# Two attentions re-ordered by pairs of heads, with the mixture product unmasked and its bias rows on VectorE

## The chip, the cores and the metric

One core of a Trainium2 chip runs the whole kernel in one launch. The metric is the device time of that launch in microseconds, lower is better. The engines that matter are TensorE (PE; PEld is its weight load), VectorE (DVE), ScalarE (ACT), GpSimd (POOL), and SyncE's queue (SPq), which issues the loads. Each engine runs its own instruction list in order, and waits on semaphores that the others raise.

## The reference, cut to what matters

A chain of eight layers over a matrix x of 256 rows and 768 columns: four graph layers and four feed-forward layers. Two of them hold an attention of 12 heads, 64 wide. Layer L0_ffn mixes attention and a cheap path by row:

```python
normed = _ln(hidden_states, g1, b1)
scores = sigmoid(normed @ Wr + br)
_, idx = top_k(-scores, 38); attn_mask[idx] = True
q, kk, v = (normed @ W + b for each)
probs = softmax(q @ kk.T / 8); ctx = probs @ v
attn_out = ctx @ Wo + bo
pooled = (scores / sum(scores)) @ normed
mix_out = (normed + scores[..., None] * pooled) @ Wm + bm
merged = where(attn_mask, attn_out, mix_out)
h = hidden_states + merged
h = h + gelu(_ln(h, g2, b2) @ W1 + bf1) @ W2 + bf2
```

L3_ffn, the last layer, has the same attention for all rows, with low-rank additions to q, k and v, then one projection whose result is added to x.

## The kernel before, in words

The 256 rows are two halves m=0, 1 of 128 partitions. Every weight product is done in three passes on rounded parts: a weight tile (128x768) is copied by ScalarE into its upper part WH (`feed_act`, L294), VectorE subtracts to get the lower part WL (`feed_vec`, L301), and activations have upper and lower parts in XS or GS (L481 on ScalarE, L485 on VectorE). There are four places for such tiles (NPAIR = 4). `ahead(i)` feeds up to tile i+4, and a place is free when PE has used it up. Raw tiles come three at a time (a unit) from SyncE's queue in a fixed order, into six buffers. A chunk of 256 output columns takes two tiles, and for each half m it is a unit of 6 x 3 matmuls.

Stage L0_ffn runs: transposes, query and key products (`pe_gemm_T`), the scores of head pairs 0 and 1, the mask's row and columns (mrow, mT) by PE, the value product (`pe_gemm_N`, tiles fv to fv+5), the attention (`pair_pe`, `pair_act`, `pair_vec`: one instruction order for each engine), the output product "om" (tiles fom to fom+11), layer norm, and the two feed-forward products. Of the eight PSUM banks, scores have 0 to 3, the turned exponentials 4 and 5, the context 6, and the spread of the reciprocals 7. `bank_at` makes PE wait until a bank's last content has been read.

For pair i of heads: `pair_scores` (PE, 8 instructions); minima of the scores (they are computed negated) by VectorE, `pair_least` (L1368); `pair_exp` (ScalarE, L1337) with the row sums in `rs`; `turn_p` (PE transposes, L363), copies of the turned halves by ScalarE (L474) and VectorE (L477); reciprocals of the sums (L1387), times the mask in L0 (L1390); `spread` (PE, L1304), which lays them along the rows; `mix` (PE, L1316), the product with the values; `ctx` (L1379), their product; then its upper (L481) and lower part (L485). The order on PE for step i is

```python
turn_p(i); spread(i)
if i + 2 < 6: pair_scores(a, i + 2, ...)
if i: mix(i - 1)
```

On VectorE it is reciprocal i, lower i-2, copy i, minima i+2, ctx i-1; on ScalarE copy i, rows i, exponentials i+2, upper i-1.

The masks: the reciprocals are multiplied by the mask column, so that the attention half is zero in rows that don't want it. The mixture mixT is multiplied by the inverse mask's row mrow on GpSimd (L1694), which also makes its lower part (L1696). "om" is one sum in PSUM for each chunk: mixture half (GS), a product of the two mask columns mT (2 partitions) with the two bias rows, and attention half (XS). VectorE adds it to xn3 (L1669).

Of the kernel before, what the change touches and what calls it, by code (L numbers as in the profile page):

```python
# [5 lines left out]
P = 128  # L6
# [148 lines left out]
def build(nc, dr, out, qgr):  # L155
    ctx = ExitStack()
    with ctx:
# [1109 lines left out]
        class Pairs:  # L1267


            def __init__(self, name, E, PT, RB, CT):  # L1270
                self.name, self.RB, self.CT = name, RB, CT
                self.E = [t.rearrange("p (h m n) -> p h m n", h=2, m=2) for t in E]
                self.PT = [t.rearrange("p (h k n) -> p h k n", h=2, k=2) for t in PT]
                self.least = [sm((name, "least", i), 4) for i in range(2)]
                self.rs = [sm2((name, "rs", i), 2) for i in range(2)]
# [11 lines left out]
        def pair_pe(a, qTv, kTv, vv, free):  # L1287
# [11 lines left out]
            def spread(i):  # L1299
                b = bank_at(7, (n + "rb", i), (act, n + "rb", i))  # L1300
                T.wait_ge(vec, n + "rs", i)
                for m in range(2):
                    for h in range(2):
                        ins = T.e.matmul(b[64 * h:64 * h + 64, m * P:(m + 1) * P],  # L1304
                                         a.rs[i % 2][:, m, h:h + 1].broadcast_to((P, 64)), ident,
                                         start=True, stop=True, skip_group_check=True)
                ins.then_inc(*pe(n + "rb", i))
# [12 lines left out]
            for i in range(6):  # L1320
                turn_p(i)
                spread(i)
                if i + 2 < 6:
                    pair_scores(a, i + 2, qTv, kTv, free)
                if i:
                    mix(i - 1)
            mix(5)

        def pair_exp(a, i):
            n = a.name  # L1330
            A.wait_ge(vec, n + "least", i)
            if i >= 2:
                A.wait_ge(pe, n + "tp", i - 2, 1)
            for h in range(2):
                bv = ps(n + "sc", i, h).rearrange("p (m n) -> p m n", m=2)
                for m in range(2):
                    A.e.activation(a.E[i % 2][:, h, m, :], bv[:, m, :], ACT.Exp, bias=a.least[i % 2][:, 2 * h + m:2 * h + m + 1],  # L1337
                                   scale=-1.0, accum_out=a.rs[i % 2][:, m, h:h + 1]).then_inc(*act(n + "E", i, h, m))

        def pair_act(a, beside):  # L1340
            n = a.name

# [4 lines left out]
            for i in range(6):  # L1347
                A.wait_ge(pe, n + "tp", i, 0)
                if i >= 2:
                    A.wait_ge(pe, n + "mix", i - 2)  # L1350
                act_copy(a.PT[i % 2][:, 0, :, :], two(ps(n + "tp", i, 0)), n + "pt", i)
# [3 lines left out]
                act_copy(a.RB[i % 2], ps(n + "rb", i)[:, 0:256], n + "rb", i)  # L1355
                if i + 2 < 6:
                    pair_exp(a, i + 2)
                if i:
                    upper(i - 1)
# [11 lines left out]
        def pair_vec(a, keep=None):  # L1371
# [12 lines left out]
            for i in range(6):  # L1384
                r = a.rs[i % 2]
                V.wait_ge(act, n + "E", i, 1, 1)
                V.e.reciprocal(r, r).then_inc(*vec())  # L1387
                if keep is not None:
                    V.wait_ge(vec)
                    V.e.tensor_tensor(r, r, keep.broadcast_to((P, 2, 2)), ALU.mult).then_inc(*vec())  # L1390
                vec.also(n + "rs", i)
                if i >= 2:
                    lower(i - 2)
                V.wait_ge(pe, n + "tp", i, 1)
                if i >= 2:
                    V.wait_ge(pe, n + "mix", i - 2)
                vec_copy(a.PT[i % 2][:, 1, :, :], two(ps(n + "tp", i, 1)), n + "pt", i)
                if i + 2 < 6:
                    pair_least(a, i + 2)
                if i:  # L1400
                    ctx(i - 1)
# [12 lines left out]
        mrow = wk(2304, n=256)  # L1414
        mT = wk(2816, n=256)
# [7 lines left out]
        def l0ffn_sync():  # L1423
# [3 lines left out]
            load_row("f0bom", 768, (pe, "sel2", 31, 2), parts=2)  # L1427
# [3 lines left out]
        def l0ffn_pe():  # L1431
# [22 lines left out]
            mk2 = sm("mk2", 4)  # L1454
            T.wait_ge(vec, "mk2")
            b = bank_at(4, ("mrow",), (vec, "mrow"))
            for m in range(2):
                ins = tr(b[:, m * P:(m + 1) * P], mk2[:, 2 * m + 1:2 * m + 2].broadcast_to((P, P)))
            ins.then_inc(*pe("mrow"))
            b = bank_at(5, ("mT",), (vec, "mT"))  # L1460
            for m in range(2):
                ins = mm(b[0:2, m * P:(m + 1) * P], [(mk2[:, 2 * m:2 * m + 2], ident)])
            ins.then_inc(*pe("mT"))
            turn[0] = 6
            pe_gemm_N("f0v", fv, 6, 512, xs_at, lambda c, m: (vec, "f0v", c, m))
            turn[0] = 4
            pe_gemm_N("f0v", fv + 4, 6, 256, xs_at, lambda c, m: (vec, "f0v", c, m), c0=512)
            T.wait_ge(vec, "f0v", 512, 1)
            pair_pe(att0, f0qA, f0kA, f0vA, there)
            turn[0] = 0  # L1470
            i = fom
            for c in range(0, 768, 256):
                h = c % 512
                if h == 0:
                    ob = [bank(("om", c, m), (vec, "hx", c, m)) for m in range(2)]
                for part_ in range(2):
                    T.wait_ge(lo, "w", i + 1)
                    if part_ == 0:
                        T.wait_ge(pool, "lower", "mix")
                    wh, wl = (v.rearrange("p (t k c) -> p t k c", t=2, k=6) for v in (w_hi(i, 2), w_lo(i, 2)))  # L1480
                    for m in range(2):
                        o = ob[m][:, h:h + 256]
                        ms = slice(m * P, (m + 1) * P)
                        for k in range(6):
                            if part_:
                                T.wait_ge(vec, "lower", "f0ctx", k)
                            x = (xs_at if part_ else gs_at)(k)
                            ins = mm(o, three_N(wh[:, :, k, :], wl[:, :, k, :], (x[0][:, ms], x[1][:, ms])),
                                     part_ == 0 and k == 0, part_ == 1 and k == 5, True)
                        if part_ == 0:  # L1490
                            T.wait_ge(*row_sem("f0bom"))
                            T.wait_ge(vec, "mT")
                            ins = mm(o, [(mT[0:2, ms], row("f0bom")[0:2, c:c + 256])], False, False, True)
                        ins.then_inc(*pe("om", c, part_, m))
                    for j in (i, i + 1):
                        pe.also("w", j)
                    i += 2
# [35 lines left out]
        def l0ffn_act():  # L1533
# [22 lines left out]
            feed_act(ahead(fv + 4))  # L1556

            def beside(i):
                if i == 2:
                    A.wait_ge(pool, "mix")  # L1560
                    act_upper(GSv[:, 0, :, :], mixT, "mix")
# [5 lines left out]
            affine_act("nT1", "f0g2", "f0b2", (pe, "om", 512, 1, 1))  # L1567
# [9 lines left out]
        def l0ffn_vec():  # L1577
# [41 lines left out]
            for m in range(2):  # L1619
                vec_gemm(fk, 2 * m + 2, None, 2 * m)  # L1620
# [10 lines left out]
                V.e.tensor_reduce(rk[:, m:m + 1], Gt, AX.X, ALU.add).then_inc(*vec())  # L1631
            mkv = mk2.rearrange("p (m a) -> p m a", m=2)
# [3 lines left out]
            vec_gemm(fk, 6, None, 4)  # L1636
            for k in range(6):
                V.wait_ge(vec, "pooled")
                V.e.scalar_tensor_tensor(out=mixT[:, k, :], in0=srow, scalar=pooled[:, k:k + 1], in1=nT[:, k, :],
                                         op0=ALU.mult, op1=ALU.add).then_inc(*vec("mixT", k))  # L1640
# [7 lines left out]

            feed_vec(ahead(fv))
            pair_least(att0, 0)  # L1650
            pair_least(att0, 1)
            V.wait_ge(pe, "mrow")
            V.e.tensor_copy(mrow, ps("mrow")[:, 0:256]).then_inc(*vec("mrow"))
            V.wait_ge(pe, "mT")
            V.e.tensor_copy(mT[0:2, :], ps("mT")[0:2, 0:256]).then_inc(*vec("mT"))
# [4 lines left out]
            pair_vec(att0, mkv[:, :, 0:1])  # L1660
            for c in range(0, 768, 256):
                feed_vec(ahead(fom + c // 256 * 4))
                feed_vec(ahead(fom + c // 256 * 4 + 2))
                if c:
                    c0 = c - c % 512
                    for m in range(2):
                        V.wait_ge(pe, "om", c, 1, m)
                        V.wait_ge(pool, "lower", "mix")
                        V.e.tensor_tensor(hx[:, m, c0:c + 256], ps("om", c0, m)[:, 0:c + 256 - c0], xn3[:, m, c0:c + 256],  # L1669
                                          ALU.add).then_inc(*vec("hx", c0, m))  # L1670
            vec_ln("f0c", hx, xn3, D, lambda m: V.wait_ge(vec, "hx", 512, m))
            affine_vec("nT1", "f0g2", "f0b2", (pe, "om", 512, 1, 1))
# [16 lines left out]

        def l0ffn_pool():  # L1690
            G.wait_ge(vec, "f0v", 512, 1)
            G.wait_ge(vec, "mixT", 5)
            G.wait_ge(vec, "mrow")
# [1488 lines left out]
```

## Time and profile before

| what | us |
|---|---|
| median of 3 runs | 1433.06 (1428.75 to 1434.76) |
| profiled execution, its own time | 1437.31 |
| its span in the trace | 1435.4 |
| PE busy | 1342.3 |
| DVE busy | 970.9 |
| ACT busy | 775.6 |
| POOL busy | 207.1 |

The span is what the trace covers; the execution's own time has a little around it. Busy time of one engine says how much of the span it works, not whether it sets the end. The first attention lies at about 545 to 590 us of the span, its output product at 590 to 621, and the last attention at 1379 to 1418.

### The profile page before, as it was taken

To read this page: it belongs to the slowest core of one execution; us is meant where nothing else is said; L and a number is where in the kernel's file an instruction comes from. 1 tells how busy PE (TensorE), PEld (TensorE's weight loads), DVE (VectorE), ACT (ScalarE), POOL (GpSimd) and SP (SyncE) were. 2 spreads that over 40 slices of the span, in tenths; PEclk is the share of its full clock that TensorE was granted. 3 is DMA by queue.
4 is the path that set the end of the run, shared out by engine and by line. 5 is a ranking of instruction groups with operands and counts; after the bars stand their busy time and mean duration, and the time that the engine had idled before them with its cause. 6 is when DMAs were issued, how large, how long until landed. Compare 5 with 4: busy or idle time off the path is not lost.

```text
span 1435.4 us, 24144 instructions
## 1 busy us (share of the span) xinstructions
PE 1342.3 (94%) x10078; PEld 1152.6 (80%) x10078; DVE 970.9 (68%) x1703; ACT 775.6 (54%) x1259; POOL 207.1 (14%) x103
## 2 busy tenths in 40 slices
PE   9999999999999889888799999789999999998798
PEld 8999543799633587787698999769899999987786
DVE  8745777745777767566667767776677767767454
ACT  3445888535888555454545554634445554436344
POOL 0110776100586200002001000001000000000100
PEclk9999999999999999999899999899999999998899
DMA  9456364135464123045233453063454555132200
GB/s 355 108 199 189 99 188 122 67 132 166 132 188 131 61 84 121 1 152 199 90 153 135 159 184 133 23 242 129 139 196 167 178 191 194 67 158 96 78 1 23
DMA packets 30835, 194.82 MB, mean 136 GB/s; under 512 B 4211, under 2 KB 4339, under 8 KB 14726
## 3 DMA queue, kind: packets, MB, share of 16 engines
q1 hardware_dynamic: 30726, 193.27, 39.6%
q8 instruction: 80, 1.31, 0.4%
q14 instruction: 29, 0.24, 0.1%
HBM read 183.03 MB, written 3.93 MB: 130 GB/s over the span
## 4 chain that ended last, share of the span: by engine, by line
PE 73%; DVE 15%; ACT 6%; POOL 3%; issue 2%; DMA 0%; DVEq 0%; SPq 0%; ACTq 0%
PE PS L358 56%; PE PS L979 6%; PE PS L988 5%; PE PS L363 3%; DVE WL L301 3%; POOL WK L1174 2%; PE PS L619 1%; POOL WL L308 1%; DVE SM L535 1%; ACT WH L294 1%; ACT WK L1337 1%; DVE GS L485 1%; ACT GS L481 1%; DVE WK L1810 1%; DVE WK L2683 1%
## 5 line engine op out<-in xcount | busy, mean ns | idle before, releaser
L301 DVE TENSOR_TENSOR WL<-w,WH 128x768 fp32r<-128x768 f32 x373 | 356.6, 967 | 204.2 <-ACT WH L294 201.3
L294 ACT ACTIVATE WH<-w 128x768 fp32r<-128x768 f32 x381 | 315.6, 840 | 256.4 <-PE PS L358 242.4
L358 PE MATMUL PS<-XS,WH 128*128 128x256 f32 x2292 | 420.8, 286 | 14.5 <-DVE XS L485 7.4
L358 PEld LDWEIGHTS PS<-XS,WH 128*128 128x128 f32 x2292 | 358.4, 191 | 18.8 <-issue 11.4
L358 PE MATMUL PS<-XS,WL 128*128 128x256 f32 x1146 | 325.6, 284 | 0.0
L358 PEld LDWEIGHTS PS<-XS,WL 128*128 128x128 f32 x1146 | 219.3, 191 | 0.0
L1112 DVE TENSOR_TENSOR WK<-PS,WK 128x1024 f32<-128x1024 f32 x128 | 156.6, 1223 | 55.5 <-ACT PS L1056 54.5
L1174 POOL TENSOR_TENSOR WK<-WK 128x1024 f32<-128x1024 f32 x64 | 152.6, 2388 | 207.9 <-ACT WK L1053 207.9
L358 PE MATMUL PS<-WH,GS 128*128 128x256 f32 x864 | 161.1, 284 | 4.6 <-issue 1.4
L1056 ACT ACTIVATE PS<-PS 128x1024 f32<-128x1024 f32 x128 | 129.5, 1011 | 34.3 <-PE PS L979 34.3
L358 PEld LDWEIGHTS PS<-WH,GS 128*128 128x128 f32 x864 | 135.9, 190 | 7.7 <-issue 4.5
L979 PE MATMUL PS<-RT,PK 128*128 128x512 f32 x384 | 122.6, 427 | 0.2
L358 PE MATMUL PS<-WL,GS 128*128 128x256 f32 x432 | 122.3, 283 | 0.0
L979 PEld LDWEIGHTS PS<-RT,PK 128*128 128x128 f32 x384 | 62.3, 188 | 71.4 <-DVE WK L1112 54.0
L358 PE MATMUL PS<-WH,XS 128*128 128x256 f32 x552 | 109.7, 285 | 1.8 <-DVE XS L485 1.8
L1982 POOL TENSOR_TENSOR XT<-XS 128x512 f32<-128x512 f32 x9 | 13.4, 1522 | 667.0 <-DVE XS L485 667.0
L988 PE MATMUL PS<-WK,cp 128*32 128x384 f32 x1024 | 107.9, 497 | 1.5 <-POOL WK L1174 1.4
L358 PEld LDWEIGHTS PS<-WH,XS 128*128 128x128 f32 x552 | 88.2, 188 | 4.4 <-issue 3.3
L358 PEld LDWEIGHTS PS<-WL,GS 128*128 128x128 f32 x432 | 82.0, 190 | 0.0
L363 PE MATMUL PS<-cp,WK 128*128 128x128 f32 x332 | 56.9, 306 | 24.7 <-ACT WK L1785 9.4
L363 PEld LDWEIGHTS PS<-cp,WK 128*128 128x128 f32 x332 | 41.7, 156 | 44.3 <-ACT WK L1785 10.9
L358 PE MATMUL PS<-WK 64*128 64x256 f32 (+4 forms) x356 | 68.9, 374 | 3.0 <-ACT WK L474 2.2
(271 smaller groups left out, 2000.3 us busy)
## 6 DMA issues: line engine op xcount, KB each, us to landing
w<-f2W_in SPq DMA_DIRECT2D x40, 1152.0 KB, 5.5
w<-Wrel_in SPq DMA_DIRECT2D x12, 1152.0 KB, 7.3
WK<-qrep_in SPq DMA_DIRECT2D x16, 768.0 KB, 5.6
w<-f1Wi_in SPq DMA_DIRECT2D x8, 1152.0 KB, 5.1
w<-f1Wo_in SPq DMA_DIRECT2D x8, 1152.0 KB, 5.1
w<-f3Wqkv_in SPq DMA_DIRECT2D x6, 1152.0 KB, 14.1
RT<-qg_rows SPq DMA_DIRECT2D x16, 384.0 KB, 6.4
RT<-AS SPq DMA_DIRECT2D x32, 192.0 KB, 6.6
```

Of the source, the lines that this page charges most:

```text
L294: A.e.activation(w_hi(i), w_raw(i), ACT.Copy).then_inc(*hi("w", i))
L301: V.e.tensor_tensor(w_lo(i), w_raw(i), w_hi(i), ALU.subtract).then_inc(*lo("w", i))
L308: G.e.tensor_tensor(w_lo(i), w_raw(i), w_hi(i), ALU.subtract).then_inc(*log("w", i))
L358: ins = T.e.matmul(o, l, r, start=i == 0 and first, stop=i == n - 1 and last, skip_group_check=lint)
L363: return T.e.transpose(o, i, ident[0:n, 0:n])
L481: A.e.activation(h, src, ACT.Copy).then_inc(*act("upper", *name))
L485: V.e.tensor_tensor(l, src, h, ALU.subtract).then_inc(*vec("lower", *name))
L979: ins = T.e.matmul(o, PK[:, j * P:(j + 1) * P], GR[b % 2][:, c:c + 512], start=True, stop=True)
L988: ins = T.e.matmul(o[32 * g:32 * (g + 1), 0:384], zsum[:, 28 - 4 * j:60 - 4 * j], SG[p % NSG][:, u, 384 * g:384 * (g + 1)], start=j == 0, ...
L1056: A.e.activation(SP[q], SP[q], ACT.Sigmoid).then_inc(*act("sig" + n, p, q))
L1112: V.e.tensor_tensor(SG[p % NSG][:, q // 2, 0:1024], SP[q], GQ[p // 4 % 2][:, 0:1024], ALU.mult).then_inc(*vec("prod" + n, p, q))
L1174: G.e.tensor_tensor(s, s, GQ[p // 4 % 2][:, 1024:1536].unsqueeze(1).broadcast_to((P, 2, 512)), ALU.mult).then_inc(*pool("prod" + n, p, 1))
```

## The change

In both attentions: PE does the scores of pair i+2 ahead of the turn of pair i; the third chunk of the value product lies between turn 0 and spread 0, with scores 2 ahead of turn 0; VectorE has the reciprocals and the minima at the head of a step; ScalarE has exponentials i+2 ahead of the rows' copy; the sums have three buffers instead of two. In L0 besides: mrow and mT are gone, and the mixture is not masked, but its product (omB, with one part ahead of the last `mix` and the rest behind it) is multiplied by the mask column when VectorE reads it from PSUM. Its upper and lower parts are made by ScalarE and VectorE before the attention, and GpSimd has no work there. The attention half (omA) has PSUM banks of its own. The bias rows are two rows broadcast to all partitions, which VectorE multiplies by the mask columns and adds. The host packs the mixture's weights ahead of the attention's.

```diff
@@ pair_pe
-            for i in range(6):
+            pair_scores(a, 2, qTv, kTv, free)
+            turn_p(0)
+            rest_v()
+            spread(0)
+            for i in range(1, 6):
+                if i + 2 < 6:
+                    pair_scores(a, i + 2, qTv, kTv, free)
                 turn_p(i)
                 spread(i)
-                if i + 2 < 6:
-                    pair_scores(a, i + 2, qTv, kTv, free)
-                if i:
-                    mix(i - 1)
+                if i == 1:
+                    T.wait_ge(vec, n + "v", 512, 1)
+                mix(i - 1)
+                beside(i)
             mix(5)
@@ pair_act
+            rows(0)
+            for i in range(1, 6):
+                pair_copy(a, i)
                 if i + 2 < 6:
                     pair_exp(a, i + 2)
-                if i:
-                    upper(i - 1)
+                rows(i)
+                upper(i - 1)
                 beside(i)
@@ pair_vec
+            for i in range(1, 6):
+                pair_shares(a, i, keep)
+                if i + 2 < 6:
+                    pair_least(a, i + 2)
+                pair_out(a, i)
                 if i >= 2:
                     lower(i - 2)
-                ...
+                ctx(i - 1)
+                beside(i)
@@ l0ffn_sync
-            load_row("f0bom", 768, (pe, "sel2", 31, 2), parts=2)
+            L.wait_ge(pe, "sum2", 31, 1)
+            L.e.dma_start(bo, dr["f0bo"].partition_broadcast(P)).then_inc(*row_sem("f0bom")[0]())
+            load_row("f0bom", 768)
@@ l0ffn_pe (beside(5) is mixed(0, 0))
-            mk2 = sm("mk2", 4)
-            ... (mrow and mT by PE)
+            pair_pe(att0, f0qA, f0kA, f0vA, there, rest_v, beside)
+            mixed(256, 0)
+            mixed(512, 2)
+            for c in range(0, 768, 256):
+                om("omA", fom + 6, c, 4 if c < 512 else 6, xs_at, lambda c, m: (vec, "hx", c, m),
+                   lambda k: T.wait_ge(vec, "lower", "f0ctx", k))
@@ l0ffn_act (beside(5) is feed_act(ahead(fom)))
+            for k in range(0, 6, 2):
+                A.wait_ge(vec, "mixT", k + 1)
+                act_upper(pair_of(GSv, 0, k), mixT[:, k:k + 2, :], "mix", k)
@@ l0ffn_vec
+            rank(0)
+            for f in range(6):
+                vec_gemm(fk, f + 1, None, f)
+                V.wait_ge(vec, "pooled")
+                V.e.scalar_tensor_tensor(out=mixT[:, f, :], in0=srow, scalar=pooled[:, f:f + 1], in1=nT[:, f, :],
+                                         op0=ALU.mult, op1=ALU.add).then_inc(*vec("mixT", f))
+            rank(1)
+            ...
+            pair_least(att0, 0)
             feed_vec(ahead(fv))
-            pair_least(att0, 0)
             pair_least(att0, 1)
+            for k in range(0, 6, 2):
+                vec_lower(pair_of(GSv, 1, k), mixT[:, k:k + 2, :], pair_of(GSv, 0, k), "mix", k)
             feed_vec(ahead(fv + 2))
             v_out(0, 512)
+            pair_least(att0, 2)
+            pair_shares(att0, 0, mkv[:, :, 0:1])
             feed_vec(ahead(fv + 4))
+            pair_out(att0, 0)
             v_out(512, 768)
+            pair_vec(att0, beside, mkv[:, :, 0:1])
+            feed_vec(ahead(fom + 2))
+            biases(0)
+            biases(1)
+            feed_vec(ahead(fom + 4))
+            V.wait_ge(vec)
+            mixed_out(0, 512)
+            feed_vec(ahead(fom + 6))
+            mixed_out(512, 768)
+            feed_vec(ahead(fom + 8))
+            om_out(0, 512)
+            feed_vec(ahead(fom + 10))
+            om_out(512, 768)
@@ biases
+            def biases(m):
+                V.wait_ge(*row_sem("f0bom"))
+                for a, b, x in ((0, bo, xn3), (1, row("f0bom")[:, 0:768], hx)):
+                    V.wait_ge(vec)
+                    V.e.scalar_tensor_tensor(out=hx[:, m, :], in0=b, scalar=mkv[:, m, a:a + 1],
+                                             in1=x[:, m, :], op0=ALU.mult, op1=ALU.add).then_inc(*vec())
@@ l0ffn_pool (whole function removed)
@@ l1gnn_sync
             load_row("g1br2", 768, (vec, "f0v", 512, 1))
-            load_row("g1be2", 768, (pe, "om", 512, 0, 1))
+            load_row("g1be2", 768, (pe, "omA", 512, 1))
             load_units(w1 + 10)
```

## Rows read from the trace of the kernel before

**Rows 1.** The page: busy time of each engine, and the last chain by engine.
```profile
PE 1342.3 (94%) x10078; PEld 1152.6 (80%) x10078; DVE 970.9 (68%) x1703; ACT 775.6 (54%) x1259; POOL 207.1 (14%) x103
PE 73%; DVE 15%; ACT 6%; POOL 3%; issue 2%; DMA 0%; DVEq 0%; SPq 0%; ACTq 0%
```
**Rows 2.** Busy time by stretches: stretch, length, engines, PE's granted clock, DMA.
```profile
554.10:589.70 35.60, 28.70 (x215) 20.37 (x213) 22.38 (x37) 17.45 (x52) 6.86 (x2) 0.86 0.15 53
589.70:620.50 30.80, 30.80 (x231) 27.96 (x230) 13.44 (x17) 11.28 (x15) 0.00 (x0) 1.00 0.10 32
1394.40:1418.00 23.60, 20.20 (x177) 13.47 (x177) 13.10 (x27) 14.38 (x49) 0.00 (x0) 1.00 0.01 2
```
**Rows 3.** PE's timeline, first attention: start, length, [idle before, releaser].
```profile
544.68 0.43 PE L363 MATMUL PS<-cp,SM 128*128 128x128 f32 x2
...
545.57 0.39 PE L358 MATMUL PS<-WH,XS 128*128 128x256 f32 x1
...
559.16 1.09 PE L363 MATMUL PS<-cp,WK 128*128 128x128 f32 x8 [0.52 <-DVE WK L1646]
562.68 1.12 PE L1304 MATMUL PS<-cp,SM 128*64 128x128 f32 x8 [2.43 <-DVE SM L1390]
563.73 2.08 PE L358 MATMUL PS<-WK 64*128 64x256 f32 x8
...
582.88 1.12 PE L1304 MATMUL PS<-cp,SM 128*64 128x128 f32 x8 [2.04 <-ACT WK L474]
```
**Rows 4.** Busy time by short stretches, first attention; PE's granted clock is third last.
```profile
558.00:560.00 2.00, 1.48 (x14) 1.28 (x12) 1.28 (x3) 0.15 (x1) 0.82 (x1) 1.00 0.32 126
...
562.60:564.00 1.40, 1.32 (x10) 0.99 (x12) 0.62 (x2) 0.15 (x1) 0.01 (x1) 0.50 0.00 0
```
**Rows 5.** Timelines of VectorE and of GpSimd, first attention.
```profile
559.22 3.40 DVE L1390 TENSOR_TENSOR SM<-SM 128x4 f32<-128x4 f32 x1
...
580.47 2.26 DVE L1390 TENSOR_TENSOR SM<-SM 128x4 f32<-128x4 f32 x1
...
559.18 3.42 POOL L1694 TENSOR_TENSOR WK<-WK 128x1536 f32<-128x1536 f32 x1 [80.12 <-DVE SM L1387]
```
**Rows 6.** The chain that ended last, at both attentions: start, length, what.
```profile
589.81 30.74 PE PS L358 x228
...
1402.06 1.93 ACT WK L1337 x8
...
1405.36 1.14 DVE SM L1368
...
1406.52 1.93 ACT WK L1337 x8
...
1418.05 13.03 PE PS L358 x108
```
**Rows 7.** PE's timeline, last attention: scores, mix, and the next scores.
```profile
1399.62 1.13 PE L358 MATMUL PS<-WK 64*128 64x256 f32 x8
1400.69 1.08 PE L1316 MATMUL PS<-WK 128*64 128x256 f32 x8
...
1403.31 1.13 PE L358 MATMUL PS<-WK 64*128 64x256 f32 x8
```
**Rows 8.** Groups by line and shape, whole span: busy us, mean ns.
```profile
L301 DVE TENSOR_TENSOR WL<-w,WH 128x768 fp32r<-128x768 f32 x373 | 356.6, 967 | 204.2 <-ACT WH L294 201.3
L294 ACT ACTIVATE WH<-w 128x768 fp32r<-128x768 f32 x381 | 315.6, 840 | 256.4 <-PE PS L358 242.4
...
L2188 DVE SCALAR_TENSOR_TENSOR WK<-WK,SM,r 128x768 f32<-128x768 f32 x2 | 1.9, 1014 | 0.0
```
**Rows 9.** Timelines of SyncE's queue and of ScalarE, around the output product.
```profile
523.50 14.19 SPq L320 DMA_DIRECT2D w<-f0Wom_in  x3
...
616.10 0.33 SPq L339 DMA_DIRECT2D r<-g1be_in  x1
...
638.00 0.83 ACT L294 ACTIVATE WH<-w 128x768 fp32r<-128x768 f32 x1
```

More of the change, by code:

```diff
@@ L1337, in pair_exp, with pair_copy, rows @@
                     A.e.activation(a.E[i % 2][:, h, m, :], bv[:, m, :], ACT.Exp, bias=a.least[i % 2][:, 2 * h + m:2 * h + m + 1],
-                                   scale=-1.0, accum_out=a.rs[i % 2][:, m, h:h + 1]).then_inc(*act(n + "E", i, h, m))
+                                   scale=-1.0, accum_out=a.rs[i % 3][:, m, h:h + 1]).then_inc(*act(n + "E", i, h, m))
+        def pair_copy(a, i):
+            n = a.name
+            A.wait_ge(pe, n + "tp", i, 0)
+            if i >= 2:
+                A.wait_ge(pe, n + "mix", i - 2)
+            act_copy(a.PT[i % 2][:, 0, :, :], two(ps(n + "tp", i, 0)), n + "pt", i)
         def pair_act(a, beside):
             n = a.name
-            def upper(i):
-                A.wait_ge(vec, n + "ctx", i)
-                act_upper(XSv[:, 0, i, :], a.CT[i % 2], n + "ctx", i)
[L1347 to L1351, printed above, removed]
+            def rows(i):
                 A.wait_ge(pe, n + "rb", i)
@@ L1463, in l0ffn_pe @@
-            ins.then_inc(*pe("mT"))
             turn[0] = 6
             pe_gemm_N("f0v", fv, 6, 512, xs_at, lambda c, m: (vec, "f0v", c, m))
[L1466 to L1469, printed above, removed]
-            turn[0] = 0
[L1471 to L1497, printed above, removed]
@@ L1556, in l0ffn_act @@
             feed_act(ahead(fv + 4))
+            pair_copy(att0, 0)
+            pair_exp(att0, 2)
             def beside(i):
-                if i == 2:
-                    A.wait_ge(pool, "mix")
-                    act_upper(GSv[:, 0, :, :], mixT, "mix")
+                if i == 5:
+                    feed_act(ahead(fom))
             pair_act(att0, beside)
@@ L1618, in l0ffn_vec, with rank @@
             V.e.tensor_copy(scol, ps("scol")[:, 0:256:128]).then_inc(*vec("scol"))
-            for m in range(2):
-                vec_gemm(fk, 2 * m + 2, None, 2 * m)
+            def rank(m):
                 sc = scol[:, m:m + 1]
@@ L1656, in l0ffn_vec, with beside @@
             feed_vec(ahead(fv + 2))
             v_out(0, 512)
+            pair_least(att0, 2)
+            pair_shares(att0, 0, mkv[:, :, 0:1])
             feed_vec(ahead(fv + 4))
+            pair_out(att0, 0)
             v_out(512, 768)
[L1660 to L1670, printed above, removed]
+            def beside(i):
+                if i == 5:
+                    feed_vec(ahead(fom))
@@ L1688, in l0ffn_vec @@
             vec_gemm_N("f0d", fw1 + 3, 3, 768, down)
[L1690 to L1693, printed above, removed]
-            G.e.tensor_tensor(mixT, mixT, mrow.unsqueeze(1).broadcast_to((P, 6, 256)), ALU.mult).then_inc(*pool("mix"))
-            G.wait_ge(act, "upper", "mix")
-            G.e.tensor_tensor(GSv[:, 1, :, :], mixT, GSv[:, 0, :, :], ALU.subtract).then_inc(*pool("lower", "mix"))
         class Gat:
@@ L3015, in pool_program @@
             l0gnn_pool()
-            l0ffn_pool()
             l1gnn_pool()
```

129 lines of the change are left out of this document (76 added, 53 removed).

## The prediction

> **What bounds the kernel now.** I read the page first: TensorE (PE) is busy 94% of the span and carries 73% of the chain that ended last [rows 1]. So a microsecond counts only where PE waits, where it runs slowly, or where it has instructions that the change takes away. Next the busy time by stretches [rows 2]. The first attention takes 35.6 us from the end of value columns 0 to 511 to the start of its output product. PE is busy for 28.7 of them at a mean granted clock of 0.86. The output product behind it is PE alone for 30.8 us, at clock 1.00. The last attention takes 23.6 us, 20.2 busy, at 1.00. The two attentions run the same code, so the last one shows what the first would cost without its extra trouble.
>
> PE's timeline of the first attention shows that trouble [rows 3]: 0.52 us for the last value evacuation, 2.43 us for the tiny masked multiply of L1390, then eight score matmuls in 2.08 us where the last attention needs 1.07 (start to start, [rows 7]), and later 2.04 us for an exponential and its copies. The granted clock behind the first idle stretch is 0.50, the 1.2 GHz level; it is 1.00 before the stretch [rows 4]. The multiply of 128x4 elements took 3.40 us, while GpSimd ran its 3.42 us product of the mixture; another took 2.26 us under GpSimd's second pass [rows 5].
>
> The chain shows the steady loop of the last attention [rows 6]: exponentials at 1402.06, minima at 1405.36, exponentials again at 1406.52. One pair costs 4.46 us and the chain goes around through ScalarE and VectorE: exponentials, upper part, lower part, copy of the turned half, minima, exponentials. PE's own instructions for a pair (scores, mix, turn, spread) take 1403.31 - 1399.62 = 3.69 us, of which the scores are 1.07 [rows 7].
>
> **Part 1, mask row and mask columns off PE.** The transposes and small products for mrow and mT begin at 544.68 and the value product at 545.57 [rows 3]. They go: 0.9 us. The value product then needs tile fv+3 two units of 2.17 us later (part 2), at 549.0. ScalarE makes that tile's upper part behind the mixture's three upper copies of 128x512, each about two thirds of the 0.84 of a 128x768 copy [rows 8], 1.7 us together; I get 547.4 for it, and 548.3 for VectorE's lower part, with the second rank (2.4 us) and the first minima ahead of it. This is hidden with 0.7 us to spare, and costs up to 0.7 if the order slips by twice that. The mixture's three lower parts on VectorE, two thirds of 0.967 each, come behind that tile, under the value product, where both engines have gaps. The row of bo and that of bm are loaded around 505, and the queue's next weight loads were at 523.5 anyway [rows 9], so the new wait ahead of them has nothing urgent behind it.
>
> **Part 2, the first attention.** PE's work: six pairs of 3.69 less the two scores done before, 6 x 3.69 - 2 x 1.07 = 20.0 us. One 128x256 unit of a weight product is 13.03 / 6 = 2.17 us at full clock [rows 6], so value columns 512 to 767, now between turn 0 and spread 0, are 4.3. Spread 0 takes bank 7, which the value product of m=1 has just left: its evacuation costs the same 0.5 us as before. No other wait remains if the loop is PE's. I followed one step of the new order with the rows' times, from the start of scores i+2 at 0. PE ends scores at 1.07, turn at 2.1, spread at 2.7, mix i-1 at 3.7. VectorE has the minima at 2.3, its copy at 2.9, ctx at 4.15. ScalarE has the exponentials from 2.35 to 4.3, rows at 4.6, upper at 4.95, and its next copy can't start before 5.3, when turn i+1 has a half. ScalarE is busy about 3.1 and VectorE about 2.7 us per step, PE 3.7. The circle of before is cut since minima stand ahead of the copy and of the lower part, and scores a turn earlier. The last mix hides its bank wait behind 4.3 us of mixture product. So the stretch from 554.2 (545.57 and four units of 2.17) to 589.7, 35.5 us, becomes 4.3 + 20.0 + 0.5 = 24.8: a gain of 10.7. Included are the clock loss (eight matmuls at 2.08 instead of 1.07, and their like) and GpSimd's hold on VectorE, since GpSimd has nothing here any more. What remains idle is as short as in the last attention, where the clock stayed 1.00.
>
> **Part 3, the output product.** It took 30.74 us [rows 6] for twelve units and six bias rows. Twelve units are 2 x 13.03 = 26.1, so the bias rows were 4.7 us and go. In their place VectorE gets four 128x768 operations with a scalar, 1.01 us each by the nearest row [rows 8]; the nearest below is the plain subtraction of 0.967. They depend on each other, so 4.2 us together. Where they lie: from the end of the last mix, ctx and upper take 0.9, ScalarE's two tiles 1.6, VectorE has its two tiles at 3.5, the biases until 7.7, and tiles fom+6, fom+7 until 9.6. PE needs them after two chunks, 8.6. It waits 1.0 us ahead of the attention half. Bounds: 0 if ScalarE and VectorE are a little quicker, 1.5 if each bias costs 1.15. After it VectorE's queue (two evacuations, each under the 1.01 us of 768 columns, and two tiles of 0.967 per chunk of 4.3) keeps ahead. The tail after the last matmul is as before: one 128x256 addition, then the statistics. Gain 3.7.
>
> The row load of g1be2 now waits for the very last unit. It went at 616.10, some 4.3 us ahead of the product's end; the weights of the next layer are queued behind it. Their first tile is used at 638.00 [rows 9], 17.4 us after that end, and such a load lands in 6 to 8 us. It is hidden; without that cover it could cost up to 4.3.
>
> **Part 4, the last attention.** Before: 23.6 us. After: 20.0 for the pairs, 0.5 for bank 7 at spread 0, 0.5 ahead of the last mix, whose bank waits for ctx 4 with nothing to put between: 21.0. Its value columns move but cost the same. Gain 2.6.
>
> **Sum.** 0.9 + 10.7 + 3.7 + 2.6 = 17.9 us. The profiled execution took 1437.3 us (span 1435.4), so 1419.4. The median of the runs shown is 1433.06, 0.3% below the profiled one; scaled by that, 1415.2.
>
> **Rule against it.** The loop still changes banks between short groups of matmuls with waits of about 0.5 us. In the last attention 3.4 us of idle time in such waits left the clock at 1.00 [rows 2]. The Trainium skill (TensorE: Matmul & The Clock Gate, section "A second HAM failure mode: psum-queue depth-cycling") says that short idle times between groups, bank after bank, can make the clock swing between its levels. This is rival B; by the rule the sum would be about 12, by the rows 17.9.
>
> **Rivals.** A: the loop stays a circle of 4.46 us (a dependence that I misjudge, say upper i-1 ahead of the next copy). Then steps 1 to 3 lose 0.77 each in both attentions, 4.6 us: gain 13, about 1420. For it: before, no middle step ran at PE's pace for long; against it: the step at 1399.62 did, as soon as minima were early. B: the clock falls once behind each of the two longer waits of the first attention (spread 0, and the 1.0 us ahead of the attention half). Rows 3 and 4 price a fall: six microseconds at half speed lose 3. Two cost 6: gain 12, about 1421. Against it: these waits are 0.5 and 1.0 us, those that were followed by a fall 2.43 and 2.04. C, slower: the clock stays at 0.50 through the first attention and its output product. This is 20 + 4.3 + 26 us of PE work, each costing as much again, 50 us at worst. It decides from 18 us of such work on, and from 25 on the kernel is slower by over 0.5%: about 1440 for 25. For it speaks only that the fall at 562.6 lasted six microseconds with PE at work; against it, the output product ran at 1.00 throughout. D: the gain is not on the end's path, so that the next stage waits for its weights: then parts 1 to 3 are cut by what the loads lag. Next-layer loads would have to be 11 us late to start to cost, and 22 to leave only 0.5%. About 1428 then.
>
> **Chances.** Forecast 0.72, A 0.12, B 0.09, C 0.02, D 0.05. A run of the kernel before varied by 0.4%, and about 0.5% is what a measurement can tell from no change. Faster by over 0.5% (below 1425.9) is the forecast, A, B: 0.93. D mostly falls within 0.5%: 0.05. Slower 0.02. The range: the low end has no wait ahead of the attention half (1.0), another microsecond of the bank waits and a median 0.3% lower (4), 1409; the high end takes in A and B, 1422.
>
> **What would show it.** No GpSimd work and no multiply over 0.2 us in 540 to 600; scores to scores 3.7 us in steps 1 to 3 of both attentions; granted clock 1.00 from the value product to the layer norm; twelve units in about 26 us with one gap of about 1 us, its releaser the lower part of a weight tile. The prediction is wrong if a step takes over 4 us, if that gap passes 2 us, or if ScalarE waits for landed weights after the stage.

## The result, and the profile after

| what | before | after |
|---|---|---|
| median, us | 1433.12 (4 runs) | 1410.34 (4 runs) |
| profiled execution | 1437.31 | 1411.12 |
| its span | 1435.4 | 1409.3 |
| mean granted clock of PE | 0.967 | 0.976 |
| PE busy | 1342.3 | 1324.7 |

The ratio is 0.9831 (95% interval 0.9809 to 0.9854): 1.7% faster, where 1.2% was forecast. 0.9831 of 1433.1 is 1408.9, just under the range's low end of 1409; the median itself, 1410.34, lies above it. A second set of six runs gave 1411.74 and 0.9866 (0.9836 to 0.9896). With all runs of this study, 80 of before (mean 1432.7, from 1424.6 to 1439.3) and 10 of the changed kernel (mean 1410.6), the gain is 22 us, give or take 2.5 (95%, from the spread of the runs). The sum said 17.9. So the direction is right and the size is some 4 us short.

Busy time by stretches of the changed kernel (stretch, length, PE, PEld, DVE, ACT, POOL, granted clock, DMA), which answers to [rows 2, 4]:

```profile
558.50:575.00 16.50, 15.95 (x152) 11.38 (x152) 11.54 (x27) 11.83 (x39) 0.00 (x0) 1.00 0.08 25
575.00:581.00 6.00, 6.00 (x50) 5.07 (x47) 2.71 (x5) 1.89 (x3) 0.00 (x0) 1.00 0.01 3
...
588.00:592.00 4.00, 3.34 (x28) 3.13 (x27) 4.00 (x6) 1.58 (x2) 0.00 (x0) 1.00 0.00 0
592.00:603.00 11.00, 11.00 (x94) 11.00 (x93) 7.29 (x11) 4.65 (x6) 0.00 (x0) 1.00 0.01 1
```

PE is busy all but half a microsecond of the loop, the clock stays at 1.00, and GpSimd has nothing. The one visible gap lies in 588 to 592. PE's timeline of the first attention, which answers to [rows 3, 7]:

```profile
558.98 0.66 PE L1304 MATMUL PS<-cp,SM 128*64 128x128 f32 x8 [0.52 <-DVE WK L1668]
559.57 1.13 PE L358 MATMUL PS<-WK 64*128 64x256 f32 x8
...
563.11 1.13 PE L358 MATMUL PS<-WK 64*128 64x256 f32 x8
...
565.68 1.03 PE L1316 MATMUL PS<-PK_,WK 128*64 128x256 f32 x8
566.65 1.14 PE L358 MATMUL PS<-WK 64*128 64x256 f32 x8
...
590.23 0.39 PE L358 MATMUL PS<-WH,XS 128*128 128x256 f32 x1 [0.66 <-DVE WL L301]
```

Spread 0 waits 0.52 us for the value evacuation, as forecast. From scores to scores is 3.54 us, less than the 3.69 counted: with the mix directly ahead of the next scores it takes 0.97 us from start to start instead of the 1.01 it took ahead of a turn, and the spread ahead of the mix takes 0.48 instead of 0.59. The wait ahead of the attention half is there, with the releaser that was named: by the spacing of its matmuls PE could have gone on at 589.4, and it did at 590.23 (the profile counts 0.66 us, from the last one's modelled end). VectorE's timeline shows why, and answers to [rows 5, 8]:

```profile
559.05 0.16 DVE L1399 TENSOR_TENSOR SM<-SM 128x4 f32<-128x4 f32 x1
...
584.26 1.01 DVE L1707 SCALAR_TENSOR_TENSOR WK<-WK,SM,XN 128x768 f32<-128x768 f32 x1
585.31 1.02 DVE L1707 SCALAR_TENSOR_TENSOR WK<-r,SM,WK 128x768 f32<-128x768 f32 x1
586.36 1.02 DVE L1707 SCALAR_TENSOR_TENSOR WK<-WK,SM,XN 128x768 f32<-128x768 f32 x1
587.42 1.02 DVE L1707 SCALAR_TENSOR_TENSOR WK<-r,SM,WK 128x768 f32<-128x768 f32 x1
588.35 1.82 DVE L301 TENSOR_TENSOR WL<-w,WH 128x768 fp32r<-128x768 f32 x2
```

The masked multiply takes 0.16 us. The four bias operations take 4.2 us, and behind them come the two tiles, ready at 590.2, that PE waits for. The chain of the changed kernel, at both attentions (start, length, what), answers to [rows 6]:

```profile
575.34 4.47 PE PS L358 x36
579.81 1.04 PE PS L1316 x8
...
590.23 13.24 PE PS L358 x108
...
1374.64 1.06 PE PS L358 x8
...
1378.17 1.06 PE PS L358 x8
...
1390.38 0.44 DVE WK L1410
1390.81 0.04 issue
1390.86 1.08 PE PS L1316 x8
```

The mixture's first part (575.34) covers what the last mix waits for in the first attention; in the last attention that wait is bare at 1390.38. The bias rows are gone from PE. In the kernel before, its timeline shows one of the six like this:

```profile
591.86 0.28 PE L358 MATMUL PS<-WH,GS 128*128 128x256 f32 x1
592.07 0.69 PE L358 MATMUL PS<-r,WK 2*128 2x256 f32 x2
592.70 0.39 PE L358 MATMUL PS<-WH,GS 128*128 128x256 f32 x1
```

The matmul ahead of it hands over 0.12 us after its start, as its neighbours do, so a bias row took 0.72 us, and six took 4.3, not the 4.7 of the forecast.

To set traces side by side I use four marks on ScalarE, its loads of function tables: ahead of the first attention (543.35 in before), behind its output product (617.76), behind the layer norm's statistics (623.50) and in the feed-forward part (643.34); and the last such load (1341.33), in the last layer, up to the span's end. Between these, in us:

| trace | 543 to 618 | 623 to 643 | 1341 to end | all the rest |
|---|---|---|---|---|
| before | 74.4 | 19.8 | 94.1 | 1247.1 |
| after | 58.9 | 18.3 | 90.8 | 1241.3 |

The first stretch gained 15.5 us and the last 3.3. The forecast had 15.3 (0.9 + 10.7 + 3.7) and 2.6. What is left, 7.3 us of 26.1, lies in places that the change doesn't touch, but for 0.1 to 0.2 us between the output product and the statistics' next mark (5.73 and 5.74 us in the traces of before, 5.60 and 5.55 in those of the changed kernel). In the feed-forward part the instructions are the same and the granted clock isn't. Here is PE alone (stretch, length, busy, granted clock, DMA), first before, then after:

```profile
628.90:632.90 4.00, 3.93 (x23) 0.65 0.24 99
```
```profile
611.80:615.80 4.00, 3.91 (x33) 1.00 1.01 414
```

23 matmuls in these 4 us at 0.65, 33 at 1.00. The question for the experiments was whether the change brings this or chance.

### The profile page after: what moved, and what is told of

Its sections match the earlier page's. It is cut to its first block, busy times and chain, and to the rows that moved or that the text cites. A ratio compares the mean times of both kernels' runs of the same rounds, so it can differ in the third digit from the quotient of the medians.

```text
span 1409.3 us, 24136 instructions
## 1 busy us (share of the span) xinstructions
PE 1324.7 (94%) x10060; PEld 1141.2 (81%) x10060; DVE 970.9 (69%) x1712; ACT 775.6 (55%) x1261; POOL 200.3 (14%) x101
## 4 chain that ended last, share of the span: by engine, by line
PE 73%; DVE 16%; ACT 6%; POOL 3%; issue 2%; DMA 0%; DVEq 0%; SPq 0%; ACTq 0%
PE PS L358 56%; PE PS L979 6%; PE PS L988 5%; DVE WL L301 3%; PE PS L363 3%; POOL WK L1174 2%; PE PS L619 2%; POOL WL L308 1%; ACT WH L294 1%; DVE SM L535 1%; DVE WK L1849 1%; ACT WK L1824 1%; DVE WK L1854 1%; DVE GS L485 1%; ACT GS L481 1%
## 5 line engine op out<-in xcount | busy, mean ns | idle before, releaser
L358 PEld LDWEIGHTS PS<-XS,WH 128*128 128x128 f32 x2292 | 355.8, 190 | 18.5 <-issue 11.1
L979 PEld LDWEIGHTS PS<-RT,PK 128*128 128x128 f32 x384 | 62.3, 188 | 71.2 <-DVE WK L1112 53.9
L358 PE MATMUL PS<-WK 128*128 128x64 f32 (+4 forms) x356 | 67.3, 366 | 3.0 <-ACT WK L474 2.2
```

What stands on the lines that cost most here:

```text
L358: ins = T.e.matmul(o, l, r, start=i == 0 and first, stop=i == n - 1 and last, skip_group_check=lint)
L979: ins = T.e.matmul(o, PK[:, j * P:(j + 1) * P], GR[b % 2][:, c:c + 512], start=True, stop=True)
```

## The experiments

Theory P: the change's own stretches give 18 to 19 us. The rest is taken to be PE's granted clock behind idle stretches elsewhere; where it is back up depends on when PE's work arrives there, not on what the change altered. Rivals: the clock is chance alone (then it averages out); or something that the change altered (loads, bank order) keeps the clock up.

**E1, E2. Both kernels again, unchanged.** No edit.

> The kernel before, unchanged, as a control. The change's own stretches explain 19 us of the 26 between the two traces; 7 us lie in stretches that it doesn't touch, where PE's granted clock rises sooner. Theory P (chance): where the clock rises differs from execution to execution. Then this trace differs from the first one of before by 1 us or more in at least one untouched stretch (the first feed-forward product behind the layer norm took 8.18 us at clock 0.79, full clock would be 6.7; the last layer's start at 1325 to 1340 ran at 0.50), and the spans of its runs spread by 4 us or more with the clock. Theory S (the change brings it): those stretches show the same clocks as in the first trace within 0.3 us, and the median stays at 1433 with the mean clock at 0.967 within 0.002.

> The changed kernel again. Theory P: mean clock of the runs 0.976 to 0.982 as before, the untouched stretches differ from the first trace of the changed kernel by 1 us or more somewhere, while value product to end of the output product stays at its 61 us within 0.3. Median 1409 to 1414. Theory S: feed-forward product at 6.67 us and the last layer's start as in the first trace, within 0.3 us.

E1: 1432.33 us (12 runs, 1425.5 to 1438.3), ratio 1.000 (0.998 to 1.002). E2: 1411.74 us (6 runs, 1405.8 to 1416.5). Stretches of E1: 73.3, 19.8, 96.5; of E2: 58.8, 18.3, 90.9. So one kernel's executions differ by over 1 us at several places, and spread by 13 us; in 35 runs of before the time is shorter where the mean clock is higher (correlation -0.91). So the clock does differ from execution to execution, as P needs, and four runs against four can't size a gain of 18 us to 2 us.

Part of the first attention's gain is such a difference. E1's first stretch is 1.1 us shorter than the first trace's. PE waits the same 2.43 us ahead of spread 0, but the spread behind the wait still runs at full speed (0.66 us, where it took 1.12), so less work falls into the slow time.

In the feed-forward stretch, 19.8 in both traces of before and 18.3 in both of the changed kernel seem to speak against chance alone. Two pairs are few, though, and elsewhere the two traces of the changed kernel don't agree. Here is PE between the same two table loads, in the first trace and in E2 (stretch, length, busy, granted clock, DMA):

```profile
746.04:768.00 21.96, 19.78 (x154) 0.92 0.24 95
```
```profile
744.25:764.65 20.40, 18.22 (x154) 1.00 0.27 103
```

The same kernel, the same 154 matmuls, 1.56 us apart.

**E3. The new order alone**, in both attentions; masks, GpSimd and output product as before.

```diff
# the changed pair_pe, pair_act, pair_vec in the kernel before; the rest of its first layer kept:
             pair_pe(att0, f0qA, f0kA, f0vA, there, rest_v, none)
             A.wait_ge(pool, "mix")        # as before, at step 2
             act_upper(GSv[:, 0, :, :], mixT, "mix")
```

> Only the new order by pairs, in both attentions; mask row, GpSimd's masking, bias rows and output product as before. My theory: steps of the pair loop at 3.5 us instead of 4.46, last attention 3.3 us shorter. In the first attention GpSimd's two passes are still there, 3.4 us each, and hold VectorE's little multiply: one wait of 1 to 3 us on PE. 1433 less 10 to 13: 1420 to 1423. Rival (the order was not what counted, only GpSimd and the bias rows did): last attention within 0.5 us of before, time 1430 or more.

1424.46 us (10 runs), ratio 0.9942 (0.9922 to 0.9962). The stretches: 69.1 in the first layer, 5 us less than in before, and 90.9 at the end, 3.2 less. GpSimd still holds VectorE up, first in the little multiply and then in the lower part of a context. PE's timeline, GpSimd's and VectorE's:

```profile
563.65 0.66 PE L1304 MATMUL PS<-cp,SM 128*64 128x128 f32 x8 [0.88 <-DVE SM L1399]
...
576.01 1.10 PE L1304 MATMUL PS<-cp,SM 128*64 128x128 f32 x8 [2.74 <-DVE SM L1399]
576.83 1.98 PE L1316 MATMUL PS<-PK_,WK 128*64 128x256 f32 x8
```
```profile
560.05 3.43 POOL L1723 TENSOR_TENSOR WK<-WK 128x1536 f32<-128x1536 f32 x1 [80.69 <-DVE SM L1396]
571.53 3.44 POOL L1725 TENSOR_TENSOR GS<-WK,GS 128x1536 fp32r<-128x1536 f32 x1 [8.05 <-ACT GS L481]
```
```profile
560.09 3.41 DVE L1399 TENSOR_TENSOR SM<-SM 128x4 f32<-128x4 f32 x1
...
571.56 3.69 DVE L485 TENSOR_TENSOR XS<-AhT,XS 128x256 fp32r<-128x256 f32 x1
...
575.70 0.16 DVE L1399 TENSOR_TENSOR SM<-SM 128x4 f32<-128x4 f32 x1
```

Two waits of 0.88 and 2.74 us, the second followed by matmuls at half speed (a mix in 1.98 us). The multiply that releases spread 4 takes 0.16 us itself. It stands behind the lower part, which took 3.69 us beside GpSimd's second pass and takes 0.41 otherwise. The order alone pays less than expected (8 to 9 us, not 10 to 13), since that pass falls where the loop has no slack.

**E4. The mixture part alone**: unmasked product, bias rows on VectorE, split output product, no GpSimd; pairs in the old order.

```diff
# the old pair_pe, pair_act, pair_vec in the changed kernel, with beside(i) at each step's end:
                 if i:
                     mix(i - 1)
+                beside(i)
             mix(5)
```

> Only the unmasked mixture, the bias rows on VectorE, the split output product, no GpSimd work; the pairs in the old order in both attentions. My theory: first attention as long as the last one of before (23.3 us of pairs), output product 26 us plus a wait of 0.8: gain 0.9 + 7.6 + 3.9 = 12.4, about 1421. No masked multiply over 0.2 us. Rival (the order is what gives the gain, GpSimd's hold would move on to another wait): under 7 us of gain, 1426 or more.

1416.52 us (6 runs), ratio 0.9900 (0.9873 to 0.9926). The first stretch is 62.3, 11 to 12 us less than before; the last is 94.1, as in before. The feed-forward stretch came out at 19.6.

**E5. Before, without GpSimd.** VectorE masks the mixture and makes its lower part. ScalarE's upper copy of the mixture moves too, from step 2 of the loop to ahead of it.

```diff
-            G.e.tensor_tensor(mixT, mixT, mrow.unsqueeze(1).broadcast_to((P, 6, 256)), ALU.mult).then_inc(*pool("mix"))
+            V.e.tensor_tensor(mixT, mixT, mrow.unsqueeze(1).broadcast_to((P, 6, 256)), ALU.mult).then_inc(*vec("mix"))
...
-            G.e.tensor_tensor(GSv[:, 1, :, :], mixT, GSv[:, 0, :, :], ALU.subtract).then_inc(*pool("lower", "mix"))
+            # at steps 2, 3, 4 of pair_vec, k = 0, 2, 4
+            V.e.tensor_tensor(GSv[:, 1, k:k + 2, :], mixT[:, k:k + 2, :], GSv[:, 0, k:k + 2, :],
+                              ALU.subtract).then_inc(*vec("lower", "mix", k))
...
-                if i == 2:
-                    A.wait_ge(pool, "mix")
-                    act_upper(GSv[:, 0, :, :], mixT, "mix")
-            pair_act(att0, beside)
+            A.wait_ge(vec, "mix")
+            act_upper(GSv[:, 0, :, :], mixT, "mix")
+            pair_act(att0, none)
```

> The kernel before with one thing changed: the mixture is masked and its lower part made by VectorE instead of GpSimd (one 128x1536 product ahead of the attention, three 128x512 subtractions in VectorE's idle time of the pair loop); the upper copy by ScalarE moves ahead of the loop. Order of the pairs, bias rows and output product as before. My theory: GpSimd's two passes cost more than half of what the mixture part gives: the 2.4 and 2.0 us waits of PE and the low clock behind them (2 to 4.5 us). From value product to the end of the output product 73.9 us becomes 66 to 68, gain 6 to 8, about 1425 to 1427; no little multiply over 0.2 us. Rival (the masked multiply was only slow because something else held VectorE, or the clock falls anyway): gain under 3, about 1431.

1425.08 us (9 runs), ratio 0.9943 (0.9924 to 0.9962): 8 us, as much as the whole new order gave, though VectorE does more. The group of the little multiplies on VectorE (count, busy, mean ns) and PE's longest wait in the loop:

```profile
L1390 DVE TENSOR_TENSOR SM<-SM 128x4 f32<-128x4 f32 x6 | 1.0, 163 | 0.2
```
```profile
568.13 0.66 PE L1304 MATMUL PS<-cp,SM 128*64 128x128 f32 x8 [0.70 <-DVE SM L1390]
```

163 ns each, where the mean of before was 1052. The first stretch is 67.3. So from 73.9 (mean of two traces of before) three steps lead down: without GpSimd 67.3, with the mixture part 62.3, with the new order 58.8: 6.5, 5.1 and 3.4 us. Each is the difference of one or two traces, and traces of one kernel differed by 1.1 us here. The 6.5 isn't GpSimd's alone: in the kernel before, ScalarE's copy of the mixture (1.49 us at 577.71) stood ahead of a copy for which PE waited 0.69 us. Up to that much, and what it cost in clock, comes from moving that copy; the two weren't tried apart.

**E6. Two of the four bias operations earlier**, at step 5 of the changed kernel.

```diff
                 if i == 5:
                     feed_vec(ahead(fom))
+                    biases(0)
...
             feed_vec(ahead(fom + 2))
-            biases(0)
             biases(1)
```

> The changed kernel with the two bias operations of m=0 moved ahead, between tiles fom+2, fom+3 and the last ctx, where VectorE was idle for 1.7 us. My theory (VectorE's four bias operations hold the tiles fom+6 and fom+7 up): the 0.66 to 0.9 us wait of PE ahead of the attention half goes, ctx 5 comes up to 0.5 us later behind cover, value product to end of output product 58.8 becomes 58.0. Rival (the wait is ScalarE's two tiles): it stays. Neither can be told by the median, 1410 to 1411; the trace decides.

1411.20 us (6 runs), ratio 0.9858 (0.9829 to 0.9887). In its chain one run of PE from 581.14 to the end of the output product has no gap:

```profile
580.13 1.01 PE PS L1316 x8
581.14 21.57 PE PS L358 x180
```

The first stretch is 57.9, 0.9 less: the four bias operations were what PE waited for. The median doesn't show it. And the feed-forward stretch came out at 19.7 instead of 18.3, with PE's clock at 0.60 at its start:

```profile
611.10:615.10 4.00, 3.96 (x21) 0.60 1.01 408
```

These are the same instructions with the same loads in the background, and more was lost there than was won.

**E7, E8. Idle matmuls behind the transposes** of six layer norms, in the changed kernel and in that of E6.

```diff
             pe_to_T("nT1", ...)
+            warm_again("f0c", 6)        # six idle matmuls in the warm-up's bank; two at five other layer norms
```

> The changed kernel with idle matmuls added behind the transposes of six layer norms, while PE waits for the parts of its input: six of about 0.44 us in the first feed-forward layer, two at five other places. Theory P: what lies outside the change's own stretches is how soon PE's clock is back up behind such idle stretches, so with the idle stretches filled it stays up more often: mean clock of the runs 0.982 or more, median 1405 to 1409. Rival (the added matmuls delay the products, or the clock falls for another reason): mean clock as before, 0.972 to 0.981, median 1411 or more.

> Both of the last two together, as a candidate that beats the changed kernel. If both theories hold: 1404 to 1408. If only the bias one: 1410.

1410.61 us (6 runs) and 1413.19 us (6 runs); mean clocks 0.975 and 0.973, no higher than the 0.977 of E2. The feed-forward stretch was 18.3 in both; in E8 that is 1.4 less than in E6, which lacks the idle matmuls. But other stretches were slow instead: the one that lies at 744 to 765 in E2, 20.40 there and in E6, took 21.93 and 21.94. Filling these small gaps isn't worth anything measurable, and this prediction of P failed. E8 doesn't beat the changed kernel.

**E9, E10, E11. Everything later by a little**: four or eight idle matmuls ahead of the first value product, in before, before and after.

```diff
+            b = bank_at(6, ("shift",), (pe, "shift"))
+            for _ in range(4):          # 8 in E10
+                ins = T.e.matmul(b[:, 0:256], ident, iota[:, 0:256], start=True, stop=True)
+            ins.then_inc(*pe("shift"))
             turn[0] = 6
             pe_gemm_N("f0v", fv, 6, 512, ...)
```

> The kernel before, with four idle matmuls (about 1.8 us of PE) ahead of the first value product: everything behind is later by that and otherwise the same. Question: the feed-forward part of the first layer, from the reciprocal root's table load behind the statistics (623.50 in the trace of before) to the next one (643.34), took 19.8 us in every trace that has before's length of the attention, and 18.3 us in four of five traces of the changed kernel. Time theory (what PE's clock does there hangs on when PE's work arrives, not on what the change altered in it): with the shift it comes out at 18.3, or at something between, though nothing in it is changed. Content theory: it stays at 19.8. Total: before plus 1.8, give or take 3 of clock.

> The same with eight idle matmuls, about 3.5 us. Time theory: the 19.8 us stretch comes out otherwise than 19.8 in this or in the run with four. Content theory: 19.8 in both.

> The changed kernel with the four idle matmuls in the same place. Time theory: the 18.3 us stretch comes out at 19.6 to 19.8, as it did where the attention was 3.4 us longer or 0.9 us shorter. Content theory: 18.3. Total: the changed kernel plus 1.8, give or take 3 of clock.

1436.75, 1435.27 (10 runs each) and 1416.29 us (4 runs): 3.7 and 2.2 us above before, and 4.6 above the changed kernel's second set, where the traces show 2.0, 3.8 and 2.0 us of added work. The feed-forward stretch: 19.8 in E9, 18.3 in E10, 19.7 in E11. So the kernel before can have the 18.3 and the changed kernel the 19.7, with nothing altered in the stretch or near it. PE's granted clock at the start of the products, E10 and then E11:

```profile
628.80:632.80 4.00, 3.90 (x33) 1.00 0.22 92
```
```profile
613.60:617.60 4.00, 3.92 (x21) 0.60 1.01 414
```

That settles one half for this stretch: what the change altered isn't needed for either value. Nor are the loads: the DMA share is 0.22 and 1.01 here, and 0.24 at clock 0.65 in before. The other half, that the arrival decides, isn't shown. Counted from the span's start the stretch begins at 623.50 in before (19.8) and at 623.43 in E10 (18.3), while in the changed kernel's two traces it begins at 606.43 and 604.11, 18.3 both times. And each shifted kernel was traced once, so chance from execution to execution is still a rival: over all 14 traces, one of seven with the old output product came out at 18.3, and four of seven with the new one.

E10 holds another such case, inside the attention. PE waits 2.04 us ahead of spread 4 as in before, where the mix behind it took 1.95 us; here it took 1.06, at clock 1.00:

```profile
584.14 0.66 PE L1304 MATMUL PS<-cp,SM 128*64 128x128 f32 x8 [2.04 <-ACT WK L474]
584.60 1.06 PE L1316 MATMUL PS<-PK_,WK 128*64 128x256 f32 x8
```

**E12. The new order in the last attention alone.**

```diff
# old pair functions for att0, the changed ones for att3; first layer as before
             pair_pe(att3, f3qA, f3kA, f3vA, there, rest_v, none)
```

> The new order in the last attention alone; the first layer is that of before. My theory: the last attention is 3.2 us shorter at full clock (loop steps 3.54 instead of 4.46), with nothing else changed; value product to the end of the output product in the first layer stays at 73 to 74.5. Median 1433 less 3, 1429 to 1431. Rival (the order also keeps PE's clock up in the last layer's products, which were 2.5 us longer in two of the four traces with the old order and in none with the new): 5 or more, 1428 or less.

1429.73 us (12 runs), ratio 0.9984 (0.9967 to 1.0001): 2 to 3 us, which the times alone don't tell from none. Its chain has the same step of 3.53 us:

```profile
1393.52 1.06 PE PS L358 x8
...
1397.06 1.06 PE PS L358 x8
```

The last stretch took 93.4 here. That is 2.6 us over the 90.8 of the changed kernel, as E1 and E5 (96.5 and 96.6) are 2.5 over before's 94.1. In E1 these 2.5 lay at 1337 to 1348, in the products ahead of the attention, at clock 0.80; in E12 the clock was 0.79 at 1330 to 1346. So they come with the new order too, which speaks against the rival, and like is to be compared with like: 94.1 to 90.8 and 96.5 to 93.4, 3.1 to 3.3 us each.

## Why the prediction was short

**Part 1** (0.9 us) was as said: the value product follows the scores at once, and tile fv+3 never holds it.

**Part 2** was forecast at 10.7 and measures 11.1: the pairs and the third value chunk take from 551.99 to 580.85 less 4.47 us of mixture product, 24.4 us instead of 35.5. About 1 us of this is chance, since in E1 the same stretch of before was 1.1 us shorter. No circle is left in the loop (rival A is out), since a step is PE's own 3.54. Two of its grounds are shown: taking GpSimd out is worth about 6.5 us (E5, with the moved copy), the order 3.4 (E4 against after). What I had not seen is that they aren't a sum: with GpSimd there, the order was worth 5 us in the first layer (E3), and without it 3.4.

One reading was wrong, with no effect on the sum. The forecast put the 2.04 us wait at 582.88 down to "an exponential and its copies". The program makes that spread wait only for bank 7, free since 579.96, and for the masked multiply. The multiply ended at 582.73, held by GpSimd's second pass, which ended at 582.71. Without GpSimd the longest such wait was 0.70 (E5).

**Part 3** was forecast at 3.7 and measures 3.6: 4.47 + 8.6 + 13.24 and a wait of 0.8 instead of 30.74. The bias rows had cost 4.3 and not 4.7. The wait of 1.0 is 0.8, and E6 shows its cause. The row load's later place cost nothing: ScalarE never waits for landed weights behind the stage.

**Part 4** was forecast at 2.6 and measures 3.3. The term that was mis-sized is the old 3.69 us for a step: in the new order it is 3.54, so the three full steps take 0.45 us less, here as in part 2. The rest is 0.25 us: the 23.6 us counted for before leave out the start of its wait for the last value columns.

**The sum.** All four measure 18.9 instead of 17.9, or 17.8 with E1 in place of the first trace. The step that failed is another. The term that was missing is the one for everything else, which stood at nothing. The sum of 17.9 held PE's clock in the untouched stretches to be the same. The runs showed that it isn't: 7.3 of the 26.1 us between the two first traces lie there, and the feed-forward stretch, at clock 0.65 at its start before and 1.00 after, gained 1.5 us in four of the six traces that have the whole change. Over all runs the untouched stretches gave 22 - 19 = 3 us, with 2.5 us of noise on the 22. Why they gained it stays open. E9 to E11 show that the change's content isn't needed for the feed-forward stretch's 1.5 us, and the two traces of the changed kernel differ by 1.56 us at 746 to 768 by themselves; whether the arrival of the work or chance sets such a step was not settled. That the other 1.5 us are of the same kind is argued from their size and not tried. The first comparison's 24 us (by the ratio) had some luck on top: the next six runs of the same kernel gave 19 to 21. Against those the forecast is 1 to 3.5 us short.

**The range.** Its low end took 4 us for the median and two for shorter waits, but put every clock effect on the slow side (rivals B and C). The clock could as well rise sooner. With a cost unknown in both directions, the range had to reach 1.5 to 3 us lower. It was missed by 0.1 us, which is less than any of these effects.

**The rule on the clock.** The Trainium skill (TensorE: Matmul & The Clock Gate, "A second HAM failure mode: psum-queue depth-cycling") would have the clock swing between groups of matmuls with short waits. In none of the traces of the changed kernel did it fall in a pair loop: waits of 0.5 and 0.8 us left it at 1.00, while in E3 a wait of 2.74 was followed by half speed. The 2.04 us wait was followed by it in before, E1, E9 and E12, and not in E10. The same page of the Trainium skill (section "What's actually happening") says that the chip watches activity on a clock of its own that doesn't start with the kernel. That fits the one wait with two outcomes, and the two traces of one kernel that differ; no run here shows it directly.

## What to carry to other kernels

Look first for a tiny instruction with a large duration: a multiply of 128x4 elements at 3.4 us beside a GpSimd pass of 3.4 us said more about the stage than its busy times, and taking the pass away was worth as much as re-ordering both loops. In a loop over several engines, put on each engine first what the next engine waits for, until a step costs the bound engine's own instructions and no more. And treat the clock behind idle stretches as a term with both signs: from one trace to the next some microseconds can be won or lost in places that an edit doesn't touch, and a small real gain (0.9 us in E6) can vanish in them.

## What the runs showed of the hardware

Two VectorE multiplies with both inputs in SBUF ended when GpSimd's pass beside them ended: one that began with it lasted 3.40 us beside 3.42, one that began later 2.26 (both ended at 582.7). The same instruction took 0.16 us without it. In E3 a subtraction of 128x256, also with both inputs in SBUF, took 3.69 us beside a pass and 0.41 otherwise. GpSimd's passes themselves took 3.4 us in every trace that has them.

The granted clock behind the idle stretch at the feed-forward part was 1.00 or 0.60 to 0.65 with the same instructions, which changes that part by 1.3 to 1.5 us. A wait of 2.04 us at one step of the first attention was followed by half speed in four traces and by clock 1.00 in one. Waits of 0.5 to 0.8 us never lowered the clock in the pair loops of the changed kernel. Executions of one unchanged kernel spread by 1%, and in 35 runs of it the time is shorter where the mean granted clock is higher (correlation -0.91).
